# Cross attention in two rounded parts per operand, head pairs on 64 rows of the array each, and a joint maximum over both heads

## What is computed

```
NUM_HEADS, HEAD_DIM = 16, 16
Q = (query @ Wq + bq), K = (key @ Wk + bk), V = (value @ Wv + bv), split into heads
scores = jnp.einsum('bhqd,bhkd->bhqk', Q, K) * scale
attn = jax.nn.softmax(scores, axis=-1)
out = jnp.einsum('bhqk,bhkd->bhqd', attn, V)
x = _layernorm(x + (out @ Wo + bo))
```

## Time and profile before

| | us |
|---|---|
| runs of the kernel before (3) | 1276.45, 1276.68, 1281.27; median 1276.68 |
| the profiled execution | 1280.25 |
| its span | 1278.4 |
| mean granted clock of TensorE | 0.956 |
| TensorE busy | 1177.9 (92%), 5844 matmuls |
| VectorE busy | 925.0 (72%) |
| ScalarE busy | 628.3 (49%) |
| GpSimd busy | 107.4 (8%) |

### The profile page before, as it was taken

One profiled execution on the slowest core, in us unless ns is written; L12 is line 12 of the kernel. 1 busy time (PEld: TensorE's weight loads), 2 busy tenths in 40 slices (PEclk: granted clock), 3 DMA queues, 4 the chain that ended last, 5 costly groups with the idle time before them and its releaser, 6 DMA issues. The chain is left out here.

```text
span 1278.4 us, 16160 instructions
## 1 busy us (share of the span) xinstructions
PE 1177.9 (92%) x5844; PEld 579.3 (45%) x5844; DVE 925.0 (72%) x1830; ACT 628.3 (49%) x1141; POOL 107.4 (8%) x94
## 2 busy tenths in 40 slices
PE   6993887799999999999999999999989989999996
PEld 3471555422323333333333332333227768888885
DVE  1317786697888878788887888878427767677675
ACT  1210222105777776777767777677783432322222
POOL 1213011500000000000000000000013410000000
PEclk9997898857999999999999999999999989999998
DMA  8000962102000000000000000000004411212120
GB/s 294 1 1 33 139 73 74 50 0 62 14 13 2 13 14 13 1 14 13 14 8 7 14 14 14 1 2 1 1 4 153 132 50 59 83 50 83 51 83 17
DMA packets 43055, 53.13 MB, mean 42 GB/s; under 512 B 4864, under 2 KB 31168, under 8 KB 42720
## 3 DMA queue, kind: packets, MB, share of 16 engines
q1 hardware_dynamic: 39104, 48.55, 14.4%
q10 hardware_dynamic: 3872, 3.56, 0.9%
HBM read 44.06 MB, written 7.83 MB: 41 GB/s over the span
## 5 line engine op out<-in xcount | busy, mean ns | idle before, releaser
L1084 DVE TENSOR_REDUCE mpart<-psum 128x1 f32<-128x400 f32 (+1 forms) x1024 | 522.9, 567 | 105.8 <-PE psum L733 101.4
L538 ACT ACTIVATE region<-psum 128x512 f32<-128x512 f32 (+1 forms) x832 | 450.2, 598 | 183.5 <-PE psum L755 182.3
L733 PE MATMUL psum<-region 96*128 96x400 bf16 (+1 forms) x1024 | 308.8, 352 | 8.7 <-DVE mpart L1084 5.6
L755 PE MATMUL psum<-region 99*128 99x512 bf16 (+1 forms) x832 | 285.0, 386 | 12.6 <-DMA region<-maxT 9.7
L766 PE MATMUL psum<-region 128*32 128x512 f32 (+1 forms) x1664 | 223.4, 609 | 0.7 <-ACT region L538 0.7
L755 PEld LDWEIGHTS psum<-region 99*128 99x128 bf16 (+1 forms) x832 | 80.6, 100 | 236.1 <-ACT region L538 186.8
L733 PEld LDWEIGHTS psum<-region 96*128 96x128 bf16 x1024 | 101.3, 99 | 181.2 <-DVE mpart L1084 132.8
L582 ACT ACTIVATE act_hi<-act_h 128x512 fp32r<-128x512 f32 x68 | 43.0, 632 | 176.0 <-DVE act_h L1260 176.0
L902 PE MATMUL psum<-x_hi,w_hi 128*128 128x512 f32 x272 | 109.9, 404 | 1.9 <-POOL w_lo L405 1.9
L903 PE MATMUL psum<-x_lo,w_hi 128*128 128x512 f32 x272 | 108.0, 397 | 0.0
L904 PE MATMUL psum<-x_hi,w_lo 128*128 128x512 f32 x272 | 108.0, 397 | 0.0
(11 more groups left out here) (148 smaller groups left out, 1027.0 us busy)
## 6 DMA issues: line engine op xcount, KB each, us to landing
blend_a<-gates_d SPq DMA_DIRECT2D x32, 256.0 KB, 3.2
blend_b<-gates_d SPq DMA_DIRECT2D x32, 256.0 KB, 3.2
region<-qparts_d SPq DMA_DIRECT2D x96, 64.0 KB, 2.2
region<-kparts_d SPq DMA_DIRECT2D x6, 800.5 KB, 28.0
qparts_d<-region SPq DMA_DIRECT2D x4, 768.0 KB, 3.5
kparts_d<-region SPq DMA_DIRECT2D x3, 800.5 KB, 5.3
xT<-in_xT SPq DMA_DIRECT2D x1, 2048.0 KB, 8.9
x_sb<-in_x ACTq DMA_DIRECT2D x1, 2048.0 KB, 24.1
```

What stands on the lines that cost most here:

```text
L538: act.activation(prob[0:r, s % 3, j, :], bank(n % ST_BANKS)[0:r], ACT.Exp).then_inc(p_ready, 1)
L733: pe.matmul(bank(MAX_BANKS[u % len(MAX_BANKS)])[:, 0:w], qstack[0:SROWS, buffer(G), j, qt * P:(qt + 1) * P], kstack[0:SROWS, g * GROUP + j ...
L755: pe.matmul(bank(n % ST_BANKS)[0:r], kstack[0:SROWS + LEVELS, g * GROUP + j, kt * P:kt * P + r], qstack[0:SROWS + LEVELS, buffer(G), j, :] ...
L1084: dve.tensor_reduce(mpart[:, u // UNITS % 2, v // PIECES, v % PIECES:v % PIECES + 1], bank(MAX_BANKS[u % len(MAX_BANKS)])[:, 0:w], X, ALU. ...
```

## The change

- Keys and queries are split into two rounded float32 parts instead of three bf16 levels, three products instead of six, so a head takes 48 rows (49 with the row of maxima, which is no longer split). `kstack`, `qstack`, `kparts_d` and `qparts_d` become float32 with half as many blocks; the bytes in SBUF stay the same. The whole `kstack` is filled with ones by GpSimd, where three rows were before.
- Two heads share a slot: one on partitions 0 to 48, one on 64 to 112. A score matmul of one lies on the upper, of the other on the lower half of the array's rows.
- A maximum unit is two matmuls of 402 columns, one for each head of a pair, into two neighbouring banks, and VectorE reads both banks with one reduction that leaves two values. 32 units for a group. The four pieces of the keys overlap by a few keys.
- Banks: 0 to 2 form a ring which is used in turn by the scores and by all the other work of a group (`extra`), with one order and one pair of semaphores; 3 holds the sums, 4 to 7 are two pairs for the maxima. ScalarE empties every slot of the ring; the turned sums and the output projection are copied to SBUF, where VectorE reads them.
- The weighted sums of step `s - 2` stand at the start of step `s`; the units stand behind score 1 and score 2 and the rest behind score 3. `LEAD` is 17 steps; the maxima are turned at step 10, the output projection at steps 7 and 8.

Two operations are left of six in each half. The core of the diff:

```diff
-SPLIT = 6
-LEVELS = 3
+SPLIT = 3
+LEVELS = 2
-Q_LEVEL = (0, 0, 0, 1, 1, 2)
-K_LEVEL = (0, 1, 2, 0, 1, 0)
-PW = -(-KEYS // PIECES)
-UNITS = TPC * GROUP * PIECES
-LEAD = KT + 3
+Q_LEVEL = (0, 1, 0)
+K_LEVEL = (0, 0, 1)
+SIDES = 2
+HALF = P // SIDES
+PAIRS = GROUP // SIDES
+PW = -(-KEYS // PIECES // 2) * 2
+UNITS = TPC * PAIRS * PIECES
+LEAD = KT + 4
+TURN_MAX_AT = 10
...
+        def extra(s):
+            G, kt = divmod(s, KT)
+            c, g = divmod(G, GROUPS)
+            if kt == TURN_MAX_AT and G + 1 < CHUNKS * GROUPS:
+                return "max"
+            if kt == 2 and G >= 1:
+                return "num"
+            if c >= 1 and g == 0 and kt in (4, 5):
+                return "attnT"
+            if c >= 1 and g == 0 and kt in (7, 8):
+                return "proj"
...
-                pe.matmul(bank(MAX_BANKS[u % len(MAX_BANKS)])[:, 0:w], qstack[0:SROWS, buffer(G), j, qt * P:(qt + 1) * P],
-                          kstack[0:SROWS, g * GROUP + j, at:at + w], start=True, stop=True).then_inc(max_scores, 1)
+                for side in range(SIDES):
+                    rows = slice(HALF * side, HALF * side + SROWS)
+                    mm = pe.matmul(bank(MAX_BANKS[u % len(MAX_BANKS)] + side)[:, 0:PW],
+                                   qstack[rows, buffer(G), p, qt * P:(qt + 1) * P],
+                                   kstack[rows, g * PAIRS + p, first_key(n):first_key(n) + PW], start=True, stop=True)
+                mm.then_inc(max_scores, 1)
...
-                pe.matmul(bank(n % ST_BANKS)[0:r], kstack[0:SROWS + LEVELS, g * GROUP + j, kt * P:kt * P + r],
-                          qstack[0:SROWS + LEVELS, buffer(G), j, :], start=True, stop=True).then_inc(st_ready, 1)
+                ring_free(n)
+                p, side = divmod(j, SIDES)
+                rows = slice(HALF * side, HALF * side + SROWS + 1)
+                pe.matmul(ring(n)[0:r], kstack[rows, g * PAIRS + p, kt * P:kt * P + r],
+                          qstack[rows, buffer(G), p, :], start=True, stop=True).then_inc(ring_full, 1)
...
+                if s >= 2:
+                    weigh(s - 2)
+                scores(s, 0)
+                scores(s, 1)
                 for u in units[0:1]:
                     max_unit(u)
-                scores(s, 0)
-                scores(s, 1)
+                scores(s, 2)
                 for u in units[1:2]:
                     max_unit(u)
-                scores(s, 2)
-                for u in units[2:3]:
+                scores(s, 3)
+                for u in units[2:]:
                     max_unit(u)
-                if s >= 1:
-                    weigh(s - 1)
-                scores(s, 3)
-                for u in units[3:]:
-                    max_unit(u)
...
-                link(dve.tensor_scalar(kf[:, f, :], kf[:, f, :], C_SCALE, None, ALU.mult))
-                link(dve.tensor_copy(kpart[:, 0, f, :], kf[:, f, :]))
-                link(dve.tensor_tensor(kres, kf[:, f, :], kpart[:, 0, f, :], ALU.subtract))
-                link(dve.tensor_copy(kpart[:, 1, f, :], kres))
-                link(dve.tensor_tensor(kres, kres, kpart[:, 1, f, :], ALU.subtract))
-                ins = dve.tensor_copy(kpart[:, 2, f, :], kres)
+                link(dve.tensor_scalar(kpart[:, 0, f, :], kf[:, f, :], C_SCALE, None, ALU.mult))
+                ins = dve.scalar_tensor_tensor(out=kpart[:, 1, f, :], in0=kf[:, f, :], scalar=C_SCALE,
+                                               in1=kpart[:, 0, f, :].bitcast(F32), op0=ALU.mult, op1=ALU.subtract)
...
                     link(dve.tensor_copy(qpart[:, 0, :], qf))
-                    link(dve.tensor_tensor(qres, qf, qpart[:, 0, :], ALU.subtract))
-                    link(dve.tensor_copy(qpart[:, 1, :], qres))
-                    link(dve.tensor_tensor(qres, qres, qpart[:, 1, :], ALU.subtract))
-                    dve.tensor_copy(qpart[:, 2, :], qres).then_inc(q_split, 1)
+                    dve.tensor_tensor(qpart[:, 1, :], qf, qpart[:, 0, :].bitcast(F32), ALU.subtract).then_inc(q_split, 1)
...
-                dve.tensor_reduce(mpart[:, u // UNITS % 2, v // PIECES, v % PIECES:v % PIECES + 1], bank(MAX_BANKS[u % len(MAX_BANKS)])[:, 0:w], X,
-                                  ALU.max).then_inc(max_read, 1)
+                dve.tensor_reduce(mpart[:, G % 2, qt, :, p, n],
+                                  bank(MAX_BANKS[u % len(MAX_BANKS)], 2).rearrange("p (b n) -> p b n", b=2)[:, :, 0:PW],
+                                  X, ALU.max).then_inc(max_read, 1)
```

More of the change, by code:

```diff
@@ L61, in buffer, with first_key @@
     return (G + 1) % GROUPS
-def piece(n):
-    at = 0 if n == 0 else PW + (n - 1) * (PW - 1)
-    return at, PW if n == 0 else PW - 1
-assert sum(piece(n)[1] for n in range(PIECES)) == KEYS and LASTK > 0
+def first_key(n):
+    return n * (KEYS - PW) // (PIECES - 1)
+assert LASTK > 0 and PW <= CHUNK
 def decoder_layer(nc, a, out):
@@ L198, in decoder_layer @@
         silu_h = sb("silu_h", [P, CHUNK])
-        blend_b = sb("blend_b", [P, 2, CHUNK])
+        blend_b = rows[:, :, :].rearrange("p (a b) n -> p a (b n)", a=2)
         blend_s = [blend_a[:, 0, :], blend_a[:, 1, :], blend_b[:, 0, :], blend_b[:, 1, :]]
@@ L249, in decoder_layer, with slot, ring, emptied @@
         STEPS = CHUNKS * GROUPS * KT
+        def extra(s):
[9 more added lines that the diff above has]
+                return "proj"
+            if c >= 1 and g == 1 and kt in (4, 5):
+                return "x2T"
+            if c >= 1 and g == 1 and kt == 6:
+                return "logits"
+            return None
+        STEP_SLOT = [1]
+        for step in range(STEPS):
+            STEP_SLOT.append(STEP_SLOT[-1] + GROUP + (extra(step) is not None))
+        def slot(s, j):
+            return STEP_SLOT[s] + j
+        def ring(n):
+            return bank(n % RING)
+        def emptied(s, j):
+            return slot(s, j) + 1
         @block.sync
@@ new lines, in turn_attn, with out_proj @@
+            def turn_attn(c, k, n):
+                pe.wait_ge(attn_ready, GROUPS * (c + 1))
+                ring_free(n)
+                for t in range(TPC):
+                    mm = pe.transpose(ring(n)[:, t * P:(t + 1) * P],
+                                      attn[:, t, 2 * k:2 * k + 2, :, :].rearrange("p g h d -> p (g h d)"), ident[:, :])
+                mm.then_inc(ring_full, 1)
+            def out_proj(c, half, n):
+                s = KT * GROUPS * (c + 1)
+                pe.wait_ge(ring_read, emptied(s + 5, GROUP))
+                ring_free(n)
+                if c == 0 and half == 0:
+                    pe.wait_ge(ld_woc, 16)
+                for q in range(2):
+                    t = 2 * half + q
+                    for k in range(DK):
+                        mm = pe.matmul(ring(n)[:, q * DIM:(q + 1) * DIM], attnT[:, k, t * P:(t + 1) * P],
+                                       wo_c[:, k, :], start=(k == 0), stop=(k == DK - 1))
+                mm.then_inc(ring_full, 1)
@@ L1167, in reads @@
                     read_max(u)
[L1168 removed]
+                    if tail_chunk is not None and tail_at + u - lo < 12 + TPC:
                         chunk_tail(tail_chunk, tail_at + u - lo)
[L1170 to L1174 removed]
+                    if u % UNITS == UNITS - 1:
+                        finish_max(u // UNITS)
             def wide(ap, n):
@@ L1276, in _ @@
                     if i == 5:
-                        for n_tail in range(11, 11 + TPC):
+                        for n_tail in range(12, 12 + TPC):
                             chunk_tail(CHUNKS - 1, n_tail)
```

448 lines of the change are left out of this document (240 added, 208 removed).

## The result

The changed kernel takes 1312.01 us in the median (1302.28 to 1328.15, four runs), the kernel before 1276.57 beside it. The ratio is 1.0245, with a 95% interval of 1.0176 to 1.0314. The forecast was 1147, its range 1088 to 1212; the sign is wrong. The profiled run of after is the shortest of the four, 1302.28, with a span of 1300.1.

The account below looks back on a forecast made before the run. TensorE was taken to set the loop, VectorE 20% below it and ScalarE 30%. From the profiled 1280.25 us, -18 before the loop and -111.5 in it gave 1150.8, 1147 against the median; range 1088 to 1212.

Parts of the forecast that it names:

- Overlap of the halves: Score and maximum matmuls: the two row halves run side by side in program order, the second starting 0.11 us behind.
- Rival (b): Loop matmuls: the halves do not overlap; group 37.2 us, kernel 1210 us; chance 0.20.
- rival (a): Loop: VectorE sets everything and never starves; group 30 us, kernel 1090 us; chance 0.13.
- Double read 0.905: VectorE's maximum reads in the loop: one read of two banks, 804 elements, costs 0.905 us; 32 cost 29.0.
- Three-unit step 3.07: Six of 13 loop steps: three reads of 0.905 us plus 0.35 for VectorE starving behind the sums, 3.07 us.
- Two-unit step 2.05: Seven of 13 loop steps: TensorE's 1.00 us of sums plus 1.05 of scores and maxima, 2.05 us.
- Last 17 steps 2.1: Steps without units at the loop's end: ScalarE's four exponentials set them, 2.1 us each instead of 2.40.
- The clock holds: TensorE's granted clock: expected to hold as only short stops are left; below 0.95 in the loop would refute it.
- Tails 6 us: Chunk tails in the loop: cost 6 of the present 8.2 us, three times, 18 us in all.
- Before the loop -18: Stages before the loop: key split -7.5, query split -9, splits between the first units -1.5; sum -18 us.
- 546 as forecast: Whole loop: 14.7 groups x 33.5 = 492, tails 18, last 17 steps 36; 546 us instead of 657.5.
- Rival (c): Loop: slower, neither overlap nor hidden weight loads; step 4.5 us, loop 930, kernel 1530 us; chance 0.08.

Follow-up runs that it names:

- e3: Changed kernel with the exponential of only 256 of the 512 columns of each score bank, so the output is not the reference's; 1255.7 us, one run.
- e1: Changed kernel with the weighted sums of step s-2 moved from the head of the step to between score 2 and score 3; 1459.51 us, ratio 1.1405.
- e9: Changed kernel with full 64-row halves, the tail two steps later, and scores going round seven banks in the last 17 steps; 1243.81 us median, ratio 0.9714.
- e8: Changed kernel with full 64-row halves and the sums split, two ahead of score 0 and two behind score 2; 1368.50 us, ratio 1.0722.
- e5: Changed kernel with each half padded to 64 rows (63 for a unit) by zero query rows, products the same; 1275.88 us, ratio 0.9968.
- e10: Changed kernel with full 64-row halves, the tail two steps later, and two unread spare maximum units in each of the last 17 steps; 1252.74 us, ratio 0.9800.
- e4: Kernel before with score and maximum matmuls contracting only 48 rows, three of six products and the row of maxima left out; 1755.42 us, one run.
- e7: Changed kernel with full 64-row halves and the chunk's tail two steps later; four runs: 1251.91, 1271.72, 1272.31 and 1272.71 us.

## Why the prediction was wrong, point by point

- *Overlap of the halves: right.* Scores 0 and 1 together take 0.50 us, one alone 0.49 (590.60, 591.84), so they start within 0.01 of each other, not the 0.11 forecast, and the two matmuls of a unit likewise. By the Trainium skill (TensorE: Matmul & The Clock Gate, Part 3) concurrent tiles start some 4 ns apart; two 0.49-us matmuls within 0.50 agree. Rival (b) is out. So is rival (a): VectorE is busy for 475.96 of the loop's 710 us and waits. But a pair is followed by the next matmul after 0.34 us, not the 0.23 forecast: the loads of the unit start 0.11 behind the scores, last 0.19, and the unit waits for them. Timeline of after, another step, with the weight loads (PEld):

```profile
605.58 0.19 PEld L842 LDWEIGHTS psum<-qstack,kstack 49*128 49x128 f32 x2 [0.84 <-ACT maxT L537]
605.59 0.50 PE L842 MATMUL psum<-qstack,kstack 49*128 49x512 f32 x2
605.69 0.19 PEld L815 LDWEIGHTS psum<-kstack,qstack 48*128 48x128 f32 x2
605.92 0.35 PE L815 MATMUL psum<-kstack,qstack 48*128 48x402 f32 x2
```

- *Double read 0.905: right* (three in 2.80 us at 591.32, one 0.99: (2.80 - 0.99) / 2). *Three-unit step 3.07: right* within 3%, and for the reason given (3.15).
- ***Two-unit step 2.05: the step that failed.*** "The sums lag two steps, so ScalarE has a step in hand; that costs nothing unless ScalarE is late". The lag gives the sums room for the weights, but it gives ScalarE no scores. How many scores it has in hand is the number of banks in the ring, three, less what TensorE holds back while 1.00 us of sums runs. The ring was described in the part on the change and never costed. Its chain is 2.67 us: e3 shows the one exponential in it, e1 the block of sums, which lengthens the chain wherever it stands, and e9 that in steps without units more banks take 2.67 down to ScalarE's own 1.96. ScalarE waits 216.0 us for scores in after, 182.3 in before (the waits of after's trace: who waits for whom, us, times, longest):

```profile
ACT region L615 <- PE psum L842: 216.0, 210, 6.8
```

  Seven two-unit steps a group at 0.62 too little are 4.3 of the 5.9 us by which a group misses, six three-unit steps 0.5, and the steps that turn the sums and the maxima most of the rest. Over 14.7 groups the term is 87 us. Not all of the 0.62 would go with a deeper ring, though: in e8, where TensorE stops nowhere in it, a two-unit step is 3.42, and without the second piece of 0.98 that is 2.4, an estimate and an upper one. So TensorE's own work was put too low as well (the 0.34 behind a pair is part of it), hidden under the ring's chain.
- *Last 17 steps 2.1: wrong by the same chain,* 2.67 at full clock, 10 us; with seven banks the forecast's figure comes out.
- ***The clock holds: the second step that failed.*** "As only short stops are left, I expect it to hold" argued from the lengths of stops alone. The rows under a matmul, 98 of a pair instead of 96 to 99 of one matmul, seemed the same on paper, but it is 98 only while both halves run, and score 3 of a two-unit step (594.99) has none beside it. With 128 rows a pair (e5) the loop's clock rises from 0.89 to 0.96, and with the later tail and the spare units (e10) the loop takes 660 us instead of 710. So the clock, and the stops of the tail that go with it, are 50 us of after's loop. That the old kernel needs its rows is shown by e4. That stops matter too is what e8 speaks for, the one kernel with full rows and almost no stops, at 1.00; and e1, at 0.67 with after's rows, says that rows are not all. Whether scores alone in their half are what matters, or the 98 of 128 rows of a pair, was not told apart.
- *Tails 6 us: too little.* With full rows and no stop for the quotient (e10) a tail group takes 45.6 us, 6.2 over a plain one, and the group behind it 3.3 more at the least (42.7); in after they cost 11 to 14 and 6 to 12, part of which is its clock. Two projections of 1.97 us and four turns, each with its slot in the same ring, are work that stays.
- *Before the loop -18: too small,* -29.7. The key split gave 9.1 (VectorE's wait for the write ends at 123.03, not at the 132.12 of the earlier trace rows), where 7.5 was forecast. The first units gave 2.7: 37.1 us from the first read, not 39.8. The query stage gave 17.9, not 9: from there to the first read it takes 103.9 us instead of 121.8, and its clock is 0.97 instead of 0.89. VectorE's busy time there falls by 12.9, just what the dropped operations were said to be worth; the other 5 us come with TensorE's higher clock, and what raised that was not tested. The two stretches, of before and of after:

```profile
132.12:253.90 121.78, 99.81 (x366) 64.01 (x367) 94.59 (x193) 27.86 (x56) 27.53 (x32) 0.89 0.49 77
```

```profile
123.03:226.90 103.87, 93.22 (x368) 60.24 (x368) 81.66 (x181) 27.71 (x56) 24.18 (x32) 0.97 0.57 99
```

The sum again with what was measured: 546 as forecast, 87 for what a group takes over 33.5, 10 in the last steps, 11 for the tails at full clock (3 x 9.5 instead of 18) make 654, where e10's loop is 660; with 50 for the clock it is after's 710. What lies before the loop gives 12 back.

Rival (c) had the right sign and put "a clock at its lower level" beside its price, but as an afterthought to another mechanism and for the whole loop. A chance of 0.08 for it was too low by the evidence at hand: the earlier trace rows already showed a stretch at 0.53 in steps with short stops.

## A version that beats both

e9 takes 1243.81 us, 0.9714 of the kernel before (0.9686 to 0.9742), and leaves nothing of the computation out. It is the changed kernel with three repairs: 64 rows in each half, the tail two steps later, seven banks where the units have ended. Its one run of 1731.92 us shows that the clock can still fail it, and counted with that run the mean of the five is 1339.6, over the kernel before; why that run stayed at 0.552 was not found, as it has no profile. With e10's spare units instead the time is 1252.74, and the longest of five runs 1254.64; five runs are too few to say that it is safe from the same.

## To carry to other kernels

Count for each ring of banks the chain that returns one: work on it, the matmul that gets it, whatever block stands between that and the next, and the latency to the consumer. If the chain is longer than the engine times you summed, it is the step, and neither a longer lag nor another place for the block helps. And when a change halves the rows that matmuls contract, treat TensorE's clock as a cost of its own: pad the rows to the full tile where zeros are free, and find the places where TensorE stops.

## What was not expected of the hardware

- Rows at work bear on the granted clock: 48 rows and a TensorE busy for 1116.36 of 1120 us ran at 0.52 (e4, one run); the same kernel with 96 to 99 rows at 0.99; the changed kernel at 0.89 with 48 and 49 rows a half and 0.96 with 63 and 64 (e5). The rows added were zeros against ones.
- With full rows too the clock can stay down while TensorE works: in e7's last group it was busy for 38.80 of 42.00 us at 0.50.
- Float32 matmuls on two column strips take as long as on four, 1.05 us (e8): a strip that is left empty is lost.
- The Trainium skill (TensorEngine Tiling (Array Packing), Key Properties) says that a change of tiling mode drains the engine. The trace fits but does not single it out: from score 3 to the sums on their strips it is 0.43 us (594.99 to 595.42), while rounded matmuls of 512 columns that follow each other start 0.23 apart; but 0.34 also pass between a pair of scores and the unit behind it, where the tiling stays the same.
